# Flamingo block, layer 1: softmax division moved from the attention output to the probabilities, on VectorE and GpSimd

## The reference

```
# layer 1, per sequence
qh = (layernorm(x) @ Wq)  -> 16 heads of 112 x 64
kh = (ctx @ Wk), vh = (ctx @ Wv) -> 16 heads of 375 x 64
scores = qh @ kh.T * 64 ** -0.5            # 112 x 375 per head
attn = softmax(scores)                     # exp(s - max) / sum
out = concat(attn @ vh) @ Wo + bo
x = x + tanh(g) * out
# then a mixture of experts on layernorm(x)
shared = silu(x @ Ws_up) @ Ws_down
top 8 of 64 experts by x @ centroids.T, weights sigmoid / sum
x = x + tanh(g) * (shared + sum over the 8 experts of w * expert(x))
```

## Time and profile before

| what | value |
|---|---|
| median of 3 runs | 2604.02 us (2601.81 to 2609.6) |
| the profiled execution: its time | 2600.7 us |
| its span | 2598.9 us |
| TensorE busy | 2383.6 us, 92% of the span |
| VectorE busy | 1746.5 us, 67% |
| ScalarE busy | 1486.8 us, 57% |
| GpSimd busy | 731.0 us, 28% |
| granted TensorE clock, mean over the span | 0.971 |

### The profile page before, as it was taken

How to read it: one execution, slowest core, us unless ns; L and a number is a source line. 1 busy time by engine, 2 the same in 40 slices (tenths; PEclk the granted TensorE clock), 3 DMA queues, 4 the chain that set the end, 5 groups by cost and what they waited for, 6 DMA issues and landing times. The chain is left out here.

```text
span 2598.9 us, 63488 instructions
## 1 busy us (share of the span) xinstructions
PE 2383.6 (92%) x20010; PEld 1793.0 (69%) x20011; DVE 1746.5 (67%) x5487; ACT 1486.8 (57%) x4483; POOL 731.0 (28%) x863
## 2 busy tenths in 40 slices
PE   5999999999997899999999999999999969999950
PEld 3777777777776566666666676666666658888850
DVE  4777777777774476777677667677767645555559
ACT  3677667667664466566566666656665514555530
POOL 2000000000000023233223323323322347777740
PEclk9999999999998999999999999999999979999975
DMA  4011011111010401111111111111111276666659
GB/s 147 22 39 39 27 39 39 27 39 39 26 34 27 141 24 45 34 46 38 36 43 38 42 37 40 45 32 46 38 37 35 74 224 185 187 189 189 186 183 381
DMA packets 148902, 203.89 MB, mean 78 GB/s; under 512 B 23784, under 2 KB 112122, under 8 KB 148642
## 3 DMA queue, kind: packets, MB, share of 16 engines
q1 hardware_dynamic: 118770, 134.56, 17.5%
q0 software_dynamic: 26544, 60.21, 6.9%
q10 hardware_dynamic: 3328, 5.77, 0.6%
HBM read 118.21 MB, written 90.61 MB: 80 GB/s over the span
## 5 line engine op out<-in xcount | busy, mean ns | idle before, releaser
L1387 ACT ACTIVATE wup<-bank,nmax 112x375 f32<-112x375 f32 x512 | 297.6, 586 | 123.4 <-DVE nmax L1491 122.1
L1982 POOL DMA_INDIRECT expert_results<-res,dest x288 | 280.6, 974 | 117.7 <-ACT res L2100 64.8
L694 ACT ACTIVATE prob<-bank,nmax 112x375 f32<-112x375 f32 x512 | 292.3, 591 | 10.0 <-DVE nmax L777 7.8
L777 DVE TENSOR_REDUCE nmax<-bank 112x1 f32<-112x375 f32 x512 | 259.6, 539 | 27.7 <-PE bank L528 27.7
L1491 DVE TENSOR_REDUCE nmax<-bank 112x1 f32<-112x375 f32 x512 | 255.1, 540 | 33.4 <-PE bank L1179 33.4
L1832 POOL DMA_INDIRECT expert_rows<-rows,ids x248 | 237.5, 958 | 78.8 <-issue 69.4
L2100 ACT ACTIVATE res<-bank,xr 128x256 f32<-128x256 f32 x288 | 136.7, 475 | 188.8 <-PE bank L2014 188.8
L1249 PE MATMUL bank<-wup,wk 128*128 128x375 f32 x512 | 223.6, 520 | 3.5 <-DVE wup L1561 2.2
L1805 POOL TENSOR_TENSOR stats<-stats,neg_half 112x1 f32<-112x1 f32 x64 | 35.8, 559 | 659.5 <-DVE stats L1522 657.2
L1393 ACT COPY pT<-bank 128x336 f32<-128x336 f32 x512 | 201.3, 450 | 19.6 <-PE bank L1186 19.1
L535 PE MATMUL bank<-ident,prob 112*128 112x112 f32 x1536 | 208.7, 262 | 4.0 <-ACT prob L694 3.7
(11 more groups left out here) (252 smaller groups left out, 5033.5 us busy)
## 6 DMA issues: line engine op xcount, KB each, us to landing
xr<-expert_rows SPq DMA_DIRECT2D x288, 129.0 KB
wup<-expert_results SPq DMA_DIRECT2D x14, 1024.0 KB, 18.8
wdn<-expert_results SPq DMA_DIRECT2D x14, 1024.0 KB, 20.3
wdn<-in_L_ffn_W_down_dram SPq DMA_DIRECT2D x8, 1024.0 KB, 12.0
expert_rows<-nowhere SPq DMA_DIRECT2D x56, 129.0 KB, 2.7
x_and_h_in<-stage SPq DMA_DIRECT2D x32, 224.0 KB, 2.4
xt<-x_and_h_in SPq DMA_DIRECT2D x32, 224.0 KB, 2.9
expert_results<-res,dest POOLq DMA_INDIRECT x288
```

The costliest lines, as they stand in the source:

```text
L694: nc.scalar.activation(prob[:, n % RING, :NK], s_bank[r][:NQ, :NK], ACT.Exp, bias=nmax[:, r:r + 1], accum_out=rsum[:, par, h:h + 1]).then_ ...
L777: nc.vector.tensor_reduce(nmax[:, r:r + 1], s_bank[r][:NQ, :NK], AX, ALU.max, negate=True).then_inc(maxed, 1)
L1387: nc.scalar.activation(prob[:, n % RING, :NK], s_bank[r][:NQ, :NK], ACT.Exp, bias=nmax[:, r:r + 1], accum_out=rsum[:, par, n:n + 1]).then_ ...
L1982: nc.gpsimd.indirect_dma_start(results_d, bass.IndirectOffsetOnAxis(ap=dest[:, n % DEST:n % DEST + 1], axis=0), res[:, n % RES, :], None, ...
```

## The change

The probabilities themselves are divided by their sums, in place, between the exponential and the turn. The reciprocal stays; `rexp`, `rT`, the four `r` pieces on TensorE and ScalarE's copies of them are gone, and the values are only copied out of their bank. VectorE divides the even heads, GpSimd the odd ones. A turn waits for the division of its head in place of the exponential. GpSimd's eight scatters are split into four pairs, one behind the divisions of each group, and the fill comes at the end of the sequence. The table and the places of VectorE's and TensorE's work are new.

```diff
-    (2, "own", "r0", "act"), (2, "post", "wo", "dve"), (3, "own", "v12", "act"), (3, "pre", "k2", "dve"),
...
+    (0, "pre", "ctxT", "dve"), (1, "post", "va3", "dve"), (3, "post", "wo", "dve"), (3, "own", "v10", "act"),
...
                 def turn(i, n):
                     wait_kept(pe, i, n - 1)
-                    pe.wait_ge(exped, H * i + n + 1)
+                    of_both = H // 2 * i + n // 2 + 1
+                    pe.wait_ge(scaled_pool if n % 2 else scaled_dve, of_both)
...
                         uses.run(hooks, i, n + 2, par, first, last)
+                        uses.run(hooks, i, n + 3, par, first, last)
                         turn(i, n + 2)
                         turn(i, n + 3)
-                        uses.run(hooks, i, n + 3, par, first, last)
...
                     nc.vector.reciprocal(rinv[:, heads], rsum[:, par, heads]).then_inc(inverted, 1)
-                    dve.wait_ge(inverted, NT * i + g + 1)
-                    freed(dve, i if g >= 2 else i - 1, f"r{(g - 2) % NT}")
-                    nc.vector.tensor_copy(rexp[:, g % 2, :].rearrange("q (h d) -> q h d", d=DK),
-                                          rinv[:, heads].unsqueeze(2).to_broadcast([NQ, 4, DK])).then_inc(expanded, 1)
...
+                def scale(i, n):
+
+                    dve.wait_ge(inverted, NT * i + n // 4 + 1)
+                    nc.vector.tensor_scalar(prob[:, n % RING, :NK], prob[:, n % RING, :NK], rinv[:, n:n + 1], None,
+                                            ALU.mult).then_inc(scaled_dve, 1)
...
-                        nc.vector.tensor_tensor(flat(oT[par][:, 2 * g:2 * g + 2, :]), misc[:, :2 * NQ], rT[:, g % 2, :],
-                                                ALU.mult).then_inc(lane_free["dve"], 1)
+                        nc.vector.tensor_copy(flat(oT[par][:, 2 * g:2 * g + 2, :]), misc[:, :2 * NQ]).then_inc(lane_free["dve"], 1)
...
-                parts_x = [(0, h_sum), (1, moments_x), (1, norm_x)]
-                parts_y = [(2, moments_y), (4, norm_y), (9, choose), (11, sigmoids), (12, weigh), (9, shared_silu),
+                parts_x = [(0, h_sum), (2, moments_x), (3, norm_x)]
+                parts_y = [(3, moments_y), (4, norm_y), (10, choose), (14, sigmoids), (14, weigh), (9, shared_silu),
                            (15, lambda p: pick(p, range(0, 2))), (14, lambda p: pick(p, range(2, 6))),
-                           (13, lambda p: pick(p, range(6, 8))), (15, place_end)]
+                           (15, lambda p: pick(p, range(6, 8))), (15, place_end)]
...
                         parts(i, n, par, first, last)
+                        scale(i, n)
                         next_maximum(i, par, n, last)
                         next_maximum(i, par, n + 1, last)
...
+                        next_maximum(i, par, n + 2, last)
+                        scale(i, n + 2)
...
                         parts(i, n + 2, par, first, last)
-                        inverses(i, par, n + 3)
+                        next_maximum(i, par, n + 3, last)
...
+                def scale(i, g):
+
+                    pool.wait_ge(inverted, NT * i + g + 1)
+                    for n in (4 * g + 1, 4 * g + 3):
+                        nc.gpsimd.tensor_scalar(prob[:, n % RING, :NK], prob[:, n % RING, :NK], rinv[:, n:n + 1], None,
+                                                ALU.mult).then_inc(scaled_pool, 1)
...
                 def body(i, par, first, last):
-                    if not last:
-                        before(i + 1, 1 - par)
+                    for g in range(NT):
+                        scale(i, g)
+                        if g == 0 and not last:
+                            before(i + 1, 1 - par)
+                        if g == 0 and not first:
+                            power(stats[:, 1, :], i - 1, y_stats, y_rstd)
+                        if i >= 2:
+                            if g == 0:
+                                weighted_rows(i - 2)
+                            scatter(range(2 * g, 2 * g + 2))
                     if not first:
-                        after(i - 1)
+                        fill(i - 1)
```

More of the change, by code:

```diff
@@ L33 @@
 ORDER_C = [
[L34 to L42 removed]
+    (0, "pre", "ctxT", "dve"), (1, "post", "va3", "dve"), (3, "post", "wo", "dve"), (3, "own", "v10", "act"),
+    (3, "pre", "k2", "dve"), (4, "pre", "k1", "act"), (4, "own", "v11", "dve"), (4, "own", "v12", "act"),
+    (5, "post", "lnT", "dve"), (5, "pre", "k3", "act"), (6, "pre", "xT", "dve"), (7, "pre", "k4", "act"),
+    (7, "own", "va0", "dve"), (8, "pre", "k0", "dve"), (8, "pre", "k6", "act"), (9, "post", "shared_up", "act"),
+    (9, "post", "router", "dve"), (10, "pre", "q0", "act"), (10, "own", "va1", "dve"), (10, "pre", "v02", "act"),
+    (11, "pre", "v00", "dve"), (12, "pre", "k5", "act"), (13, "post", "rank", "dve"), (13, "pre", "v01", "act"),
+    (14, "post", "shared_down", "dve"), (14, "pre", "q1", "act"), (15, "own", "va2", "dve"), (15, "pre", "k7", "act"),
 ]
@@ L1020, in layer1_phase @@
                        + [("xT", "q0"), ("xT", "q1"), ("va3", "wo"), ("wo", "lnT"), ("lnT", "router"), ("lnT", "shared_up"),
-                          ("router", "rank"), ("shared_up", "shared_down"), ("va0", "va1"), ("va1", "va2"), ("r0", "r1"), ("r1", "r2")]):
+                          ("router", "rank"), ("shared_up", "shared_down"), ("va0", "va1"), ("va1", "va2")]):
         assert place(one) < place(other)
@@ L1058, in layer1_phase @@
         nmax, rsum, rinv = sb("nmax", [NQ, 4]), sb("rsum", [NQ, 2, H]), sb("rinv", [NQ, H])
-        rexp, rT = sb("rexp", [NQ, 2, 4 * DK]), sb("rT", [P, 2, 2 * NQ])
         rt, rts = sb("rt", [NQ, 8, E]), sb("rts", [NQ, 16])
@@ L1261, in v @@
                     return f
-                def inverse(g):
-                    def f(p, par, n):
-                        misc = lane(f"r{g}", n)
-                        pe.wait_ge(expanded, NT * p + g + 1)
-                        for a in range(2):
-                            mm = pe.transpose(misc[:, a * NQ:(a + 1) * NQ], rexp[:, g % 2, a * P:(a + 1) * P], ident[:NQ, :NQ])
-                        left(mm, f"r{g}")
-                    return f
                 def wo(p, par, n):
@@ L1309, in _ @@
                 hooks |= {f"q{g}": q(g) for g in range(2)} | {f"k{p}": k(p) for p in range(PAIRS)}
-                hooks |= {f"v{half}{c}": v(half, c) for half in range(2) for c in range(KC)} | {f"r{g}": inverse(g) for g in range(NT)}
+                hooks |= {f"v{half}{c}": v(half, c) for half in range(2) for c in range(KC)}
                 hooks |= {f"va{g}": values(g) for g in range(NT)}
@@ L1416, in v @@
                     return f
-                def inverse(g):
-                    def f(p, par, n):
-                        misc = full(act, "act", n)
-                        freed(act, p if g >= 2 else p - 1, f"va{(g - 2) % NT}")
-                        nc.scalar.copy(rT[:, g % 2, :], misc[:, :2 * NQ]).then_inc(lane_free["act"], 1)
-                    return f
                 def tanh_h(j):
@@ L1443, in _ @@
                 hooks = {f"q{g}": q(g) for g in range(2)} | {f"k{p}": k(p) for p in range(PAIRS) if uses.lane[f"k{p}"] == "act"}
-                hooks |= {f"v{half}{c}": v(half, c) for half in range(2) for c in range(KC) if uses.lane[f"v{half}{c}"] == "act"} | {f"r{g}": inverse(g) for g in range(NT)}
+                hooks |= {f"v{half}{c}": v(half, c) for half in range(2) for c in range(KC) if uses.lane[f"v{half}{c}"] == "act"}
                 hooks |= {"router": lambda p, par, n: sigmoid_exp(p), "shared_up": shared_exps}
@@ L1458, in tanhs @@
                 def tanhs(i, n, last):
-                    if n == 0 and not last:
+                    if n == 1 and not last:
                         tanh_h(i + 1)
@@ L1642, in pick @@
                 def pick(p, ks):
+                    dve.wait_ge(routed, N_ROUTER * (p + 1))
                     for k in ks:
@@ L1704, in next_maximum @@
                         maximum(i + 1, n + 4 - H)
-                def inverses(i, par, n):
-                    for v, at in enumerate((0, 7, 8, 12)):
-                        if n == at:
-                            inverse(i, par, v)
                 def body(i, par, first, last):
@@ L1837, in before @@
                     residual_x(j, par)
-                def after(p):
-                    power(stats[:, 1, :], p, y_stats, y_rstd)
-                    if not (isinstance(p, int) and p == 0):
-                        weighted_rows(p - 1)
-                        scatter(range(TOP_K))
-                    fill(p)
+                def scale(i, g):
[3 more added lines that the diff above has]
+                                                ALU.mult).then_inc(scaled_pool, 1)
                 nc.gpsimd.iota(numbers[:], pattern=[[1, TOP_K]], base=0, channel_multiplier=TOP_K).then_inc(numbered, 1)
```

21 lines of the change are left out of this document (4 added, 17 removed).

## The result

The changed kernel takes 2629.12 us (median of 5 runs, 2619.4 to 2633.38), the kernel before 2604.02 (5 runs): ratio 1.0095, interval 1.0076 to 1.0113. It is slower by 25 us, with the sign that was forecast and inside the range of the forecast, whose middle was +40. The profiled execution took 2630.34 us with a span of 2628.3.

The account below looks back on a forecast made before the run. TensorE's instructions were taken to bound layer 1. Per sequence -1.04 + 2.05 + 0.35 = +1.36 us, +41 us over 30 sequences, two others giving back 2: 2644 us; 8-in-10 range 2570 to 2690.

Parts of the forecast that it names:

- The signs that the prediction named: Layer 1: TensorE idle 2 to 3 us a sequence before wo and second scores; picks or weigh near 1.9 us.
- GpSimd's division: Each of GpSimd's 8 divisions of 112x375 a sequence was taken at 0.7 us, bounds 0.57 and 1.07.
- The gain: TensorE loses four transposes of inverse sums, 1.04 us a sequence, 33 us over 32; nothing else there gets shorter.
- TensorE's schedule: From shared_down's start, TensorE could start wo at 8.66 us in the changed order, against 12.38 before.
- The fill holds VectorE's picks: GpSimd's 112x2048 copy locks VectorE out of SBUF at its picks for 1.86 us, 1.6 to 1.9 allowed.
- Where it meets them: Fill starts 2.66 us after shared_down, VectorE's first pick at 2.70; the second scores then wait 1.2 us.
- The second meeting: At group 0's reciprocals, GpSimd's divisions of heads 1 and 3 hold VectorE's h_sum and division: 0.6 us taken.
- Head 5 and the rest: Head 5's division behind two scatters (bounded by 0 and 0.5 us) plus release time: 0.35 us a sequence.
- Rival 3: GpSimd becomes what TensorE waits for, its division taking 1.5 us or more: 2680 to 2720 us, chance 0.11.
- ScalarE at nothing: ScalarE, 61% busy, loses four copies of turned sums and gains one k copy; counted as no cost.
- VectorE's division 0.42: Each of VectorE's 8 in-place divisions of 112x375 a sequence was taken at 0.42 us, 0.58 from above.
- the holds do not reach TensorE: Rival: fill starts earlier or VectorE has more slack, so only the gain remains: 2571 us, up to 2590, chance 0.27.

Follow-up runs that it names:

- the version with both moves: Changed kernel with the fill put behind the next sequence's first divisions and the scatters regrouped 3, 3, 2 behind groups 1, 2, 3: 2560.86 us, ratio 0.9842.
- the version with the shorter instruction: Changed kernel with fill and scatters both later, GpSimd's divisions written as two-input products with the broadcast reciprocal: 2572.12 us (one run).
- the three kernels: Third chip, kernel before: without turned sums and division, short fill, 2937.63 us; group 1's values moved behind q0, 3010.49; that move without sums and division, 2975.44.
- The one kernel of the new order that ran there: Changed kernel with fill and scatters both later, GpSimd multiplying by the constant 0.01 instead of the reciprocal: 2709.17 us (one run, third chip).

## Why the prediction was right, point by point

By the periods the change is +0.78 us a sequence: 38.56 less 37.78, times 31 is 24 us, nearly the whole difference. The version with both moves, the new order without its two waits, has 36.48 (908.5 to 2039.5). So the new order gives 1.30 and its waits take 2.08. The forecast was 1.04 and 2.40, and both terms missed in the direction that makes the change look worse, so the sum was 0.6 us a sequence too high. The signs that the prediction named came true in part: TensorE fell to 95.4% busy and a pick was held in most sequences, but no wait for an exponential appeared ahead of the second scores, and GpSimd's division is far from 0.7, which it had named as a sign of being wrong.

- **The gain**: right in size by chance, wrong in its reason. The step that failed is "Nothing else on TensorE gets shorter; the rest is reordering. If the others keep up, this is the whole gain." The transposes alone are worth 0.1 us a sequence in the old order (2599 against 2602), since the others do not keep up there: in most sequences the fill holds hs times z, and what the missing `r` pieces free is lost behind it. I had read 99.7% busy in the earlier trace rows as "TensorE waits for nothing"; the kernel before had a cost of its own from the fill, which shows as longer distances between starts. That the new order puts the fill where hs times z isn't held (0.276 in every instance) is a likely source of the gain; the turned sums put back into the new order, which would split the 1.30, wasn't tried.
- **TensorE's schedule**: shared_down to wo without a hold was worked out as 8.66 us; the median in the version with both moves is 8.72.
- **The fill holds VectorE's picks**: shown three ways, by moving it, by shortening it and by its instances. 1.86 us of hold was forecast; the 24 held picks in the trace from 900 to 2050 us last 1.73 at their median, so 1.45 more than alone. The time from shared_down to wo rose to 10.13, by 1.41; with both meetings 2.05 was forecast.
- **Where it meets them**: off. The fill came at 3.97 and not at 2.66; 1.1 of that is what two divisions on GpSimd take beyond what I gave them. The second scores therefore never waited for an exponential, and the wait stood ahead of the values instead. The end, wo late, is the same, as all of it is one queue on VectorE.
- **The second meeting** (0.6 us): right in size on VectorE, but without a price. h_sum went from 0.41 to 0.59 and the division behind it to 0.69 beside GpSimd's, some 0.5 us together. The version with both moves has the same, and from shared_down to wo it takes no longer than the kernel without divisions (8.72 both).
- **Head 5 and the rest** (0.35, head 5 bounded by 0.5): mis-sized. The stretch from the transposes of x1ln to shared_up takes 7.97 us, against 7.22 with the scatters later, and moving the scatters gave back 25 us, 0.8 a sequence. A division of 1.27 instead of 0.7 is the reason: with 0.7 the turn of head 5 could start 0.57 us sooner, and TensorE waits 0.60 for it.
- **GpSimd's division**: 1.27 us, above my upper bound of 1.07. The bound was scaled from a two-input operation, and the two-input form indeed takes 0.81; the one-input form with a scalar is the dearer, which no row of before showed. Rival 3 put its threshold at 1.5.
- **ScalarE at nothing, VectorE's division 0.42**: right; ScalarE fell to 686.73 us, and with 16 divisions VectorE still makes 2580.

The rival on the other side, "the holds do not reach TensorE", was given 2571; with the holds moved away the kernel makes 2561. In the changed kernel itself it failed, since nothing kept the fill off the picks.

## What to carry to other kernels

A bound engine that is 99.7% busy may still be waiting, and rows of waits may show only a part of what a late result costs (27.9 and 17.3 us of waits gave back 46 and 25). Compare the distances of its starts between sequences of the same run, and take the shortest as the floor, before a removed instruction is counted at its full price. When VectorE's queue is a single chain, place GpSimd's long copies by what stands in VectorE's queue at that moment, and put a transfer's issue behind the work that TensorE waits for: two such moves turned +1% into -1.6% here with nothing else changed. For GpSimd measure the very form, and what it does to VectorE beside it: the version with the shorter instruction came out 11 us slower in its one run.

## What the runs showed of the hardware

- A GpSimd copy of 112x2048 holds a two-input operation of VectorE in SBUF until it ends (picks 0.28 to 1.31 and up to 1.97 us, hs times z 0.28 to 1.94). It holds a one-input operation of VectorE in SBUF as well: in the version with both moves 29 divisions that meet it take 1.56 us instead of 0.41 and end 0.21 us after it.
- GpSimd's TENSOR_SCALAR of 112x375 holds VectorE's divisions too, but not always to its end. In the version with both moves 130 of them overlap one. 62 end 0.21 us after GpSimd's ends. 34 started first and take 0.42, and GpSimd's then takes 1.47 us instead of 1.23. But 33 that start 0.04 us behind GpSimd's are through after 0.74 us, 0.45 us before it ends. With two inputs, in 0.81 us, 117 of 124 end 0.21 us after GpSimd's ends. Beside a scatter a division takes 0.41 us as it does alone (61 and 64 instances in the changed kernel). The Trainium skill, page SBUF — State Buffer, section Who interferes with whom, has the ports locked for a whole instruction of GpSimd; that agrees with the copy and with the two-input form, and for the 33 divisions beside the one-input form it doesn't, so the measurement decides.
- GpSimd's TENSOR_SCALAR costs 1.27 us for 375 columns (3.4 ns each) with a scalar from SBUF and 1.17 with a constant, TENSOR_TENSOR 0.81, a copy 1.89 for 2048 columns (0.9 ns each).
- Chips differ. On the third one the kernel before takes 2965 us instead of 2603. Its expert stage moves a fifth less a second (142 against 183 GB/s), and in the old order three engines stop until a run of eight scatters is over. In each of the three kernels 29 such stops end 1.53 to 1.74 us after the end of a scatter. In one of the 29 a gap of 3.6 us lies between two scatters, and the engines go on in the gap:

```profile
1649.44 0.94 POOL L1827 DMA_INDIRECT expert_rows<-rows,ids  x1 [0.30 <-issue]
1651.93 0.39 DVE L1507 COPY oT<-bank 128x224 f32<-128x224 f32 x1 [6.03 <-remote]
...
1653.99 0.94 POOL L1827 DMA_INDIRECT expert_rows<-rows,ids  x1 [3.62 <-issue]
```

The one kernel of the new order that ran there has two or three scatters at a time, and its stop costs 1 us a sequence instead of 5.7. What holds the engines isn't settled (the trace calls the releaser "remote"), nor was the changed kernel itself run on that chip; pairs of scatters may be worth far more there than the 25 us that the change costs here.
